# Decoder with local attention: the last tiles of gates and values share one weight tile, the order lists are rewritten, the first stage is reordered

## The chip, the cores and the metric

One NeuronCore of a Trainium2 chip. The metric is the device time of one launch in microseconds; 2953.05 us is the median of three runs of the kernel before (2951.69 to 2956.47).

## What is computed

Eight sequences of 256 tokens by 256 channels go through three blocks, all in fp32:

```python
x = x + gelu(layernorm(x) @ W_K.T @ W1.T) @ W2.T             # memory read, 64 hidden
x = x + softmax(q k.T / 16) v                                 # cross attention: q from layernorm(x), k and v from ctx
y = layernorm(x)
for i in range(6):                                            # six layers
    y = local_attention(shift(y)) @ Wo[i] + y                 # 16 heads of 64, windows of 64, rotary, l2 norms
    a, g = split(layernorm(shift(y)) @ W1[i] + b1[i])         # 682 values and 682 gates
    y = (a * gelu(g)) @ W2[i] + b2[i] + y
x = x + y
```

682 is five tiles of 128 and a rest of 42.

## The kernel before, in words

`front` does the memory read and the cross attention in two quads of four sequences. Each step of a quad is a loop over its four sequences on each engine: transposes of the normalised rows (line 443), hidden (453), read (460), keys (468), transposes again, values (478), queries (485), scores (495), transposes of the probabilities (502), cross output (508). The layer norms are DVE work with a power taken on POOL: (0, 0), (0, 1), (1, 0), (0, 2), (1, 1), (1, 2) by quad and place, (i, 2) being the last norm of a quad, whose result is the `y` that the layers read. Beside this, the weights of layer 0 are staged in six blocks (`Weights.stage`, lines 235 to 252), split by ACT into a high part (`split_high`) and by POOL into a low part (`split_low`). All loads go through SP's queue, in the order in which SP issues them. PE begins after one semaphore, `weights_in`, has counted ten loads (line 428).

`layers` runs 48 steps (6 layers by 8 sequences) as a software pipeline of slots. A slot mixes the attention of one step, the projections of the next and the feed-forward of the one before. What each engine does in a slot is written out by hand in PE_ORDER, ACT_ORDER, DVE_ORDER and POOL_ORDER (lines 66 to 97); an engine works strictly along its list and waits on semaphores. An item of PE's list is a group of matmuls: `unit` (6 matmuls 128x512, line 884), `turn` (4 or 8 transposes, 899 to 903), `project_out` (24, line 914), `norm_turn` (924), `input` (867), `gate` and `value` (12 matmuls 128x256, line 939), `down` (12, line 954), `scores` (976), `turned` (988), `mix` (1002 to 1006). Two PSUM banks `project` take the units and turns in turn, so each waits until the one before the last was read; `wide` takes gates and values, one item after the other.

Every product is three passes (high by high, low by high, high by low). `wide` holds two tiles of 128 columns by 256 tokens; gate items 0, 1, 2 fill tiles 0 to 5 of the gates and value items 0, 1, 2 tiles 0 to 5 of the values. The sixth tile of each has 42 columns that count; the other 86 are the next columns of the weight row or padding. ACT takes the gelu of the gates (line 1085), with a table load before the first and another back to exp after the last (1129). DVE multiplies values by gates (1292), ACT and DVE split the product (1094 to 1097, 1300 to 1303) and `down` uses it.

```python
for k in range(2):
    col = (2 * i + k) * P + (FFN if kind == "gate" else 0)
    for h in range(HALVES):
        for a, w in PASSES:
            last = pe.matmul(wide[:, k, :], w_up[w][:, h * W1_COLS + col:h * W1_COLS + col + P], xnT[a][:, h, :], ...)
```

The weights of the next layer are split chunk by chunk during a layer (`chunk_split_high`, `chunk_split_low`, lines 286 and 291), stored to HBM and fetched at the change of layers (line 315).

Of the kernel before, what the change touches and what calls it, by code (L numbers as in the profile page):

```python
# [4 lines left out]
FP32 = mybir.dt.float32  # L5
# [6 lines left out]
P = 128  # L12
# [20 lines left out]
W1_COLS = 2 * FFN  # L33
W1_PAD = FFN_TILES * P - FFN
# [41 lines left out]
ACT_ORDER = [  # L76
    ("out", 3), ("unit", 1, 0), ("unit", 1, 1), ("exp", 0, 0), ("exp", 0, 1), ("unit", 1, 2), ("unit", 1, 3), ("copied", 0, 0),
    ("copied", 0, 1), ("split_high", 0, 0), ("turn", 1, 0), ("turn", 1, 1), ("split_high", 0, 1), ("exp", 1, 0), ("turn", 1, 2),
    ("out", 0), ("unit", 1, 4), ("exp", 1, 1), ("unit", 1, 5), ("turn", 1, 3), ("copied", 1, 0), ("input",), ("copied", 1, 1),
    ("norm_turn",), ("exp", 2, 0), ("unit", 0, 0), ("exp", 2, 1), ("unit", 0, 1), ("gate", 0), ("copied", 2, 0), ("out", 1),  # L80
    ("unit", 0, 2), ("gate", 1), ("unit", 0, 3), ("copied", 2, 1), ("gate", 2), ("exp_table",), ("exp", 3, 0), ("value", 0),
    ("split_high", 1, 0), ("turn", 0, 0), ("split_high", 1, 1), ("unit", 0, 4), ("out", 2), ("value", 1), ("exp", 3, 1),
    ("turn", 0, 1), ("turn", 0, 2), ("value", 2), ("copied", 3, 0), ("unit", 0, 5), ("turn", 0, 3), ("copied", 3, 1),
]
DVE_ORDER = [
    ("mask", 0, 0), ("mask", 0, 1), ("out", 3), ("rotate", 1, 0), ("rotate", 1, 1), ("scale", 0, 0), ("scale", 0, 1),
    ("rotate", 1, 2), ("rotate", 1, 3), ("add_out",), ("mask", 1, 0), ("norm_stats",), ("mask", 1, 1), ("scale", 1, 0),
    ("norm_apply",), ("scale", 1, 1), ("split_low", 0, 0), ("out", 0), ("input",), ("mask", 2, 0), ("mask", 2, 1),
    ("norm_turn",), ("scale", 2, 0), ("rotate", 0, 0), ("split_low", 0, 1), ("rotate", 0, 1), ("scale", 2, 1), ("out", 1),
    ("rotate", 0, 2), ("rotate", 0, 3), ("mask", 3, 0), ("value", 0), ("low", 0), ("value", 1), ("mask", 3, 1), ("low", 1),  # L90
    ("scale", 3, 0), ("value", 2), ("scale", 3, 1), ("low", 2), ("out", 2), ("split_low", 1, 0), ("split_low", 1, 1),
    ("residual",),
# [87 lines left out]
class Weights:  # L180
# [5 lines left out]
    def __init__(self, nc, ctx, D):  # L186
# [6 lines left out]

        self.up_flat = two("w_up", [P, HALVES * W1_COLS + W1_PAD])
        self.up = [part[:, 0:HALVES * W1_COLS].rearrange("p (k n) -> p k n", k=HALVES) for part in self.up_flat]
# [19 lines left out]
    def split_views(self, blk):  # L215
# [7 lines left out]
        if blk < 5:  # L223
            pieces = []
            for a in range(0, FFN, 2 * P):
                b = min(a + 2 * P, FFN)
                at = FFN if blk == 3 else 0
                pieces.append([(s[:, :, a:b], self.up[0][:, :, at + a:at + b], self.up[1][:, :, at + a:at + b])])
            return pieces
# [1233 lines left out]
```

## Time and profile before

| what | value |
|---|---|
| median of the runs | 2953.05 us |
| the profiled execution's own time | 2952.34 us |
| its span | 2950.6 us |
| PE, DVE, ACT, POOL busy | 94%, 78%, 67%, 46% of the span |
| mean granted TensorE clock | 0.987 |
| matmuls on line 939 (gates and values) | 3456 |

The span runs from the first instruction to the last; 1.7 us of the execution's own time lie outside it. Busy shares are per engine; a matmul's recorded duration is longer than its share of the engine, since matmuls overlap, so what a group takes is read from one start to the next.

### The profile page before, as it was taken

The numbers are of one execution on the slowest core, as the hardware profiler recorded it, in microseconds if no ns is written. First come the engines' busy times: TensorE is split into PE (matmuls) and PEld (weight loads), VectorE is DVE, ScalarE is ACT, GpSimd is POOL, SyncE is SP. The second block draws the span as 40 slices with busy tenths as digits, with TensorE's granted clock in tenths as the row PEclk, the third lists the DMA queues.
The fourth block names the chain that finished last, engine by engine and source line by source line (L and its number), as shares of the span: only waits on it lengthen the run. The fifth ranks groups of instructions, "written<-read, shape, count | busy, mean of one in ns | idle before, by whom it ended". The sixth has DMA issues, their size and how long they took to land. (4 is left out here: it accounts for less than half of the span.)

```text
span 2950.6 us, 80978 instructions
## 1 busy us (share of the span) xinstructions
PE 2779.4 (94%) x26408; PEld 2447.7 (83%) x26408; DVE 2311.7 (78%) x7881; ACT 1976.5 (67%) x5719; POOL 1363.0 (46%) x1436
## 2 busy tenths in 40 slices
PE   7769999999999999999999999999999999999996
PEld 5658888888888888888888888888888888888886
DVE  3568888887888878888887888878888887887873
ACT  4346776777677667677767767766776776676663
POOL 3354453544445445454444545545454454545440
PEclk9989999999999999999999999999999999999997
DMA  3212222333322324222144232233223232210110
GB/s 121 86 36 90 75 70 88 112 100 111 106 75 70 110 96 141 84 87 81 63 140 138 71 96 76 79 130 135 77 70 103 75 135 86 65 30 23 37 25 20
DMA packets 140063, 251.67 MB, mean 85 GB/s; under 512 B 14718, under 2 KB 78728, under 8 KB 138632
## 3 DMA queue, kind: packets, MB, share of 16 engines
q1 hardware_dynamic: 139912, 249.76, 25.8%
q8 instruction: 83, 1.36, 0.2%
q14 instruction: 68, 0.56, 0.1%
HBM read 137.72 MB, written 80.55 MB: 74 GB/s over the span
## 5 line engine op out<-in xcount | busy, mean ns | idle before, releaser
L884 PE MATMUL project<-w_qkv,xT 128*128 128x512 f32 x3456 | 892.5, 402 | 17.5 <-DVE with_sin L1254 11.3
L884 PEld LDWEIGHTS project<-w_qkv,xT 128*128 128x128 f32 x3456 | 621.9, 189 | 156.6 <-issue 13.1
L1158 POOL TENSOR_SCALAR sums_sq<-sums_sq 128x8 f32<-128x8 f32 x384 | 92.1, 240 | 1241.6 <-DVE sums_sq L1249 1236.1
L1104 ACT ACTIVATE probs<-probs,shift 128x128 f32<-128x128 f32 x1536 | 595.3, 390 | 72.7 <-DVE shift L1322 72.4
L1322 DVE CUSTOM_DVE_ANT_0 probs<-score,mask,query_scale 128x128 f32<-128x128 f32 x1536 | 439.9, 348 | 157.8 <-PE score L976 146.9
L939 PE MATMUL wide<-nT,w_up 128*128 128x256 f32 x3456 | 480.4, 289 | 13.5 <-ACT gates L1085 3.4
L939 PEld LDWEIGHTS wide<-nT,w_up 128*128 128x128 f32 x3456 | 441.0, 191 | 44.4 <-ACT gates L1085 23.7
L1334 DVE TENSOR_SCALAR probs<-probs,sums 128x128 f32<-128x128 f32 x1536 | 426.6, 341 | 13.5
L1053 ACT ACTIVATE with_sin<-project 128x512 f32<-128x512 f32 x384 | 230.1, 599 | 189.6 <-PE project L884 189.5
L1167 POOL TENSOR_TENSOR sums_sq<-sums_sq,half 128x8 f32<-128x8 f32 x192 | 321.4, 1674 | 16.0
L1164 POOL TENSOR_TENSOR query_scale<-sums_sq,half 128x8 f32<-128x8 f32 x192 | 317.7, 1654 | 22.2 <-POOL sums_sq L1158 12.3
L1111 ACT COPY probsT<-turned 128x512 f32<-128x512 f32 x384 | 224.9, 586 | 135.7 <-issue 99.8
L914 PE MATMUL acc<-w_out,oT 128*128 128x256 f32 x2304 | 295.7, 284 | 1.6 <-issue 1.6
L914 PEld LDWEIGHTS acc<-w_out,oT 128*128 128x128 f32 x2304 | 285.9, 188 | 5.9 <-issue 1.7
L1104 ACT ACTIVATION_READ_ACCUMULATOR probs<-probs,shift 128x1 f32 x1536 | 288.6, 188 | 0.0
L988 PE MATMUL turned<-ident,probs 128*128 128x128 f32 x1536 | 236.9, 277 | 41.6 <-DVE probs L1334 40.3
L1249 DVE TENSOR_REDUCE sums_sq<-with_sin 128x8 f32<-128x512 f32 x384 | 260.4, 678 | 18.9 <-ACT with_sin L1053 18.2
L1254 DVE TENSOR_TENSOR with_sin<-project,tables 128x512 f32<-128x512 f32 x384 | 260.9, 680 | 0.0
L1252 DVE TENSOR_TENSOR with_cos<-project,tables 128x512 f32<-128x512 f32 x384 | 260.9, 679 | 0.0
L1170 POOL TENSOR_TENSOR with_cos<-with_cos,with_sin 128x512 f32<-128x512 f32 x192 | 249.5, 1299 | 0.0
L1292 DVE SCALAR_TENSOR_TENSOR gates<-wide,params,gates 128x256 f32<-128x256 f32 (+1 forms) x288 | 125.9, 479 | 148.8 <-PE wide L939 148.8
L954 PE MATMUL acc<-w_down,hT 128*128 128x256 f32 (+1 forms) x1728 | 236.8, 283 | 1.8 <-DVE hT L1303 1.6
(119 smaller groups left out, 4655.7 us busy)
## 6 DMA issues: line engine op xcount, KB each, us to landing
w_parts_scratch<-staging SPq DMA_DIRECT2D x120, 519.0 KB, 3.1
staging<-in_w_next SPq DMA_DIRECT2D x60, 519.0 KB, 5.0
w_qkv<-w_parts_scratch SPq DMA_DIRECT2D x20, 1536.0 KB, 9.3
v_mid<-v SPq DMA_DIRECT2D x192, 128.0 KB, 2.3
w_up<-w_parts_scratch SPq DMA_DIRECT2D x20, 682.0 KB, 6.2
y_in<-y_scratch SPq DMA_DIRECT2D x48, 256.0 KB, 3.7
res<-y_scratch SPq DMA_DIRECT2D x48, 256.0 KB, 2.8
y_scratch<-res SPq DMA_DIRECT2D x40, 256.0 KB, 4.1
```

The lines of the kernel that those rows point to most:

```text
L884: last = pe.matmul(project[(x - 1) % 2][:], xT[a][:, h, t * P:(t + 1) * P], w_qkv[w][:, h, c, g, :], start=(h == 0 and (a, w) == PASSES[0] ...
L914: last = pe.matmul(acc[:, t, :], oT[a][:, p, t * P:(t + 1) * P], w_out[w][:, p, :], start=(p == 0 and (a, w) == PASSES[0]), stop=(p == PAI ...
L939: last = pe.matmul(wide[:, k, :], w_up[w][:, h * W1_COLS + col:h * W1_COLS + col + P], xnT[a][:, h, :], start=(h == 0 and (a, w) == PASSES ...
L1104: last = act.activation(probs[:, k, cols], probs[:, k, cols], ACT.Exp, bias=shift[:, k, i:i + 1], scale=-1.0, accum_out=sums[:, k, i:i + 1])
L1164: pool.tensor_tensor(query_scale[:, u // 2, g * GROUP_HEADS:(g + 1) * GROUP_HEADS], sums_sq[:, u, :], half[:, 0:GROUP_HEADS], ALU.pow).the ...
L1167: pool.tensor_tensor(sums_sq[:, u, :], sums_sq[:, u, :], half[:, 0:GROUP_HEADS], ALU.pow)
L1170: pool.tensor_tensor(with_cos[:, u, :], with_cos[:, u, :], with_sin[:, u, :], ALU.add).then_inc(pool_step, 1)
L1249: dve.tensor_reduce(sums_sq[:, u, :], with_sin[:, u, :].rearrange("p (h d) -> p h d", h=GROUP_HEADS), AXIS_X, ALU.add).then_inc(squares_su ...
L1252: dve.tensor_tensor(heads(with_cos[:, u, :]), heads(bank[:]), table(2 * c), ALU.mult)
L1254: dve.tensor_tensor(heads(with_sin[:, u, :]), heads(bank[:])[:, :, ::-1, :], table(2 * c + 1), ALU.mult).then_inc(parts_ready, 1)
L1322: last = dve.tensor_tensor_reduce(out=probs[:, h, a:b], in0=score[h % 2][:, at + a:at + b], in1=mask[:, a:b], scale=query_scale[:, i, head ...
L1334: last = dve.tensor_scalar(probs[:, h, a:b], probs[:, h, a:b], sums[:, h, i:i + 1], None, ALU.mult)
```

## The change

Three parts.

1. The 42 rest columns of the values and of the gates are laid side by side in one tile of 128 columns of `w_up` (values at 0, gates at 64, the gaps zeroed). `gate` 2 computes gate tile 4 and this shared tile; `value` 2 computes value tile 4 alone. ACT takes the gelu of rows 64 to 105 of the shared tile; a new DVE item `rest` multiplies rows 0 to 41 of PSUM (plus bias) by it, and only then is `wide` given back to `value` 0. The rest columns are fetched by extra DMAs (42 columns each, 20 in all), and `gate` 2 now also waits for the values' weights.
2. All lists but POOL's are rewritten.
3. `front`: the loads are reordered, three of them (`ident`, `wk_mem`, `w1t_mem`) issued by ACT and waited for alone; PE's wait for the other weights, with the mask that is the last of them, comes before the read; x arrives by one semaphore for each of the first four; contexts of the second quad are loaded as soon as the values of the first are done; layer norm (1, 0) comes before the scores of the first quad; the cross sums of a quad are interleaved with the statistics of its last norm; the splits of blocks 0, 2, 3 and 5 come after an ACT step that they came before; the first `y_in` of the layers is loaded inside `front`, the tables are built after `input`, and only one column of `xT` is cleared in each part.

```diff
-W1_COLS = 2 * FFN
+FULL = FFN - FFN_REST
+GATE_REST = 64
+W1_COLS = 2 * FULL + P
...
 PE_ORDER = [
-    ("scores", 0), ("mix", 3), ("unit", 1, 0), ("unit", 1, 1), ("project_out", 0), ("unit", 1, 2), ("unit", 1, 3),
-    ("turned", 0, 0), ("project_out", 1), ("turned", 0, 1), ("turn", 1, 0), ("turn", 1, 1),
-    ("scores", 1), ("mix", 0), ("turn", 1, 2), ("unit", 1, 4), ("unit", 1, 5), ("turn", 1, 3), ("turned", 1, 0), ("norm_turn",),
-    ("input",), ("turned", 1, 1),
+    ("scores", 0), ("mix", 3), ("unit", 1, 0), ("unit", 1, 1), ("project_out", 0), ("unit", 1, 2), ("project_out", 1),
+    ("turned", 0, 0), ("unit", 1, 3), ("turned", 0, 1), ("turn", 1, 0),
+    ("scores", 1), ("mix", 0), ("turn", 1, 2), ("unit", 1, 5), ("turn", 1, 1), ("unit", 1, 4), ("turned", 1, 0), ("turn", 1, 3),
+    ("turned", 1, 1), ("input",), ("norm_turn",),
     ("scores", 2), ("mix", 1), ("unit", 0, 0), ("unit", 0, 1), ("gate", 0), ("turned", 2, 0), ("unit", 0, 2), ("gate", 1),
     ("unit", 0, 3), ("turned", 2, 1), ("gate", 2),
-    ("scores", 3), ("mix", 2), ("value", 0), ("turn", 0, 0), ("unit", 0, 4), ("value", 1), ("down", 0), ("turn", 0, 1),
-    ("turn", 0, 2), ("value", 2), ("down", 1), ("turned", 3, 0), ("unit", 0, 5), ("turn", 0, 3), ("turned", 3, 1), ("down", 2),
+    ("scores", 3), ("mix", 2), ("value", 0), ("unit", 0, 4), ("value", 1), ("turned", 3, 0), ("turn", 0, 1), ("down", 0),
+    ("unit", 0, 5), ("value", 2), ("down", 1), ("turn", 0, 0), ("turn", 0, 2), ("turned", 3, 1), ("turn", 0, 3), ("down", 2),
 ]
...
+    ("out", 3), ("unit", 1, 0), ("exp", 0, 0), ("unit", 1, 1), ("exp", 0, 1), ("unit", 1, 2), ("split_high", 0, 0),
+    ("copied", 0, 0), ("unit", 1, 3), ("copied", 0, 1), ("turn", 1, 0), ("out", 0), ("exp", 1, 0), ("turn", 1, 2),
+    ("unit", 1, 5), ("exp", 1, 1), ("turn", 1, 1), ("unit", 1, 4), ("copied", 1, 0), ("turn", 1, 3), ("input",),
+    ("copied", 1, 1), ("norm_turn",), ("exp", 2, 0), ("unit", 0, 0), ("exp", 2, 1), ("unit", 0, 1), ("gate", 0), ("out", 1),
...
+    ("rotate", 1, 2), ("add_out",), ("rotate", 1, 3), ("mask", 1, 0), ("mask", 1, 1), ("norm_stats",), ("scale", 1, 0),
+    ("split_low", 0, 0), ("scale", 1, 1), ("norm_apply",), ("out", 0), ("input",), ("mask", 2, 0), ("mask", 2, 1),
...
+    ("rotate", 0, 3), ("rest",), ("mask", 3, 0), ("mask", 3, 1), ("value", 0), ("scale", 3, 0), ("low", 0), ("value", 1),
+    ("split_low", 0, 1), ("out", 2), ("low", 1), ("scale", 3, 1), ("value", 2), ("low", 2), ("split_low", 1, 0), ("residual",),
...
             def slot(s):
-                if s.early:
+                if s.early and not (isinstance(n, int) and n == -1):
                     wait(sp, filled, n * FILLS + 2)
...
-                    for k in range(2):
-                        col = (2 * i + k) * P + (FFN if kind == "gate" else 0)
+                    for k in range(1 if x == 7 else 2):
+                        col = (2 * i + k) * P + (FULL if kind == "gate" else 0)
...
-                    last.then_inc(wide_read, 1)
+                        rows = slice(0, P) if j < FFN_TILES - 1 else slice(GATE_REST, GATE_REST + FFN_REST)
+                        last = act.activation(gates[rows, j, :], wide[rows, k, :], ACT.Gelu,
+                                              bias=params[rows, FFN_TILES + j:FFN_TILES + j + 1])
+                    last.then_inc(wide_read if i < 2 else gated, 1)
...
+                elif kind == "rest":
+                    dve.wait_ge(params_loaded, s.layer * 32 + 32)
+                    dve.wait_ge(gated, f + 1)
+                    j = FFN_TILES - 1
+                    dve.scalar_tensor_tensor(gates[0:FFN_REST, j, :], wide[0:FFN_REST, 1, :], params[0:FFN_REST, j:j + 1],
+                                             gates[GATE_REST:GATE_REST + FFN_REST, j, :], ALU.add, ALU.mult).then_inc(wide_read, 1)
```

and in `front` (PE, SP, DVE):

```diff
-            pe.wait_ge(weights_in, 16 * 10)
+            pe.wait_ge(fold_in, 16 * 3)
...
+                if i == 0:
+                    pe.wait_ge(weights_in, 16 * 7)
...
+            W.stage(sp, 0)
+            for k in range(QUAD, BATCH):
+                sp.dma_start(x[k][:], as_tiles(D["x"][k])).then_inc(x_in[QUAD], 16)
+            sp.dma_start(T["mask"][:], D["mask"]).then_inc(weights_in, 16)
+            for blk in (1, 2):
+                W.stage(sp, blk)
+            sp.wait_ge(kv_ready, 2 * QUAD)
+            for k in range(QUAD, BATCH):
                 load_context(k)
...
+                    sp.wait_ge(y_stored, 16 * QUAD)
+                    sp.dma_start(T["y_in"][:], as_tiles(D["y"][0])).then_inc(T["y_loaded"], 16)
...
+                if i == 0:
+                    layer_norm(1, 0, lambda j: dve.wait_ge(x_in[QUAD], QUAD * 16))
...
-                if i == 0:
-                    layer_norm(1, 0, lambda j: dve.wait_ge(x_in[1], QUAD * 16))
-                layer_norm(i, 2, lambda j: dve.wait_ge(cross_added, i * QUAD + j + 1))
+                    dve.wait_ge(cross_added, k + 1)
+                layer_norm(i, 2, add_cross)
```

## Rows read from the trace of the kernel before

**Rows 1.** The page: busy time of each engine over the span.
```profile
PE 2779.4 (94%) x26408; PEld 2447.7 (83%) x26408; DVE 2311.7 (78%) x7881; ACT 1976.5 (67%) x5719; POOL 1363.0 (46%) x1436
```

**Rows 2.** Busy time by stretch, one slot of layer 2 (columns in the first line).
```profile
core 0: us, PE busy (x) PEld busy (x) DVE busy (x) ACT busy (x) POOL busy (x), PEclk, DMA share, GB/s
1218.00:1274.70 56.70, 55.22 (x542) 48.83 (x541) 47.57 (x162) 40.71 (x118) 27.05 (x28) 1.00 0.25 82
```

**Rows 3.** Timeline of PE, same slot: start, duration, line, tiles, count [idle before].
```profile
1218.01 0.60 PE L867 MATMUL project<-ident,y_in 128*128 128x128 f32 x4
...
1219.03 1.10 PE L976 MATMUL score<-kT,qT 64*64 64x128 f32 x32
...
1234.82 1.69 PE L939 MATMUL wide<-nT,w_up 128*128 128x256 f32 x12
...
1242.62 1.66 PE L939 MATMUL wide<-nT,w_up 128*128 128x256 f32 x12
1244.12 1.55 PE L954 MATMUL acc<-w_down,hT 128*128 128x256 f32 x12
...
1249.92 1.10 PE L976 MATMUL score<-kT,qT 64*64 64x128 f32 x32
...
1263.85 0.60 PE L988 MATMUL turned<-ident,probs 128*128 128x128 f32 x4
...
1265.56 0.66 PE L899 MATMUL project<-ident,with_cos 128*128 128x128 f32 x4 [0.23 <-DVE with_sin L1254]
...
1271.94 0.60 PE L899 MATMUL project<-ident,with_cos 128*128 128x128 f32 x4
1273.14 0.66 PE L988 MATMUL turned<-ident,probs 128*128 128x128 f32 x4 [0.60 <-DVE probs L1334]
1274.24 0.65 PE L924 MATMUL wide<-ident,xn 128*128 128x128 f32 x4 [0.45 <-DVE xn L1277]
1274.73 0.60 PE L867 MATMUL project<-ident,y_in 128*128 128x128 f32 x4
```

**Rows 4.** Timeline of ACT, same slot: gelu of gate 2, the first exp of `scores` 1.
```profile
1232.84 0.84 ACT L1085 ACTIVATE gates<-wide,params 128x256 f32<-128x256 f32 x2 [0.78 <-PE wide L939]
...
1268.19 0.40 ACT L1104 ACTIVATE probs<-probs,shift 128x128 f32<-128x128 f32 x1 [0.83 <-DVE shift L1322]
```

**Rows 5.** Timeline of DVE, same slot: end of the last rotation, the mask behind it.
```profile
1232.94 0.68 DVE L1254 TENSOR_TENSOR with_sin<-project,tables 128x512 f32<-128x512 f32 x1
1234.13 0.35 DVE L1322 CUSTOM_DVE_ANT_0 probs<-score,mask,query_scale 128x128 f32<-128x128 f32 x1 [0.50 <-PE score L976]
...
1234.40 0.35 DVE L1322 CUSTOM_DVE_ANT_0 probs<-score,mask,query_scale 128x128 f32<-128x128 f32 x1
```

**Rows 6.** Groups by line and form, whole span: the product of the sixth tile.
```profile
L1292 DVE SCALAR_TENSOR_TENSOR gates<-wide,params,gates 42x256 f32<-42x256 f32 x48 | 22.5, 469 | 0.0
```

**Rows 7.** Timeline of PE in `front` and at the start of `layers`.
```profile
27.05 6.42 PE L460 MATMUL fb<-w2t_mem,hidT 64*128 64x256 f32 x16 [1.89 <-ACT hidT L522]
...
69.94 7.17 PE L508 MATMUL fb<-fv,fpT 128*128 128x256 f32 x32 [1.89 <-ACT fpT L553]
81.98 3.81 PE L443 MATMUL fb<-ident,xn 128*128 128x128 f32 x16 [4.87 <-DVE xn L593]
...
100.09 8.58 PE L468 MATMUL fb<-ctxT,wk_cross 128*128 128x256 f32 x32 [6.81 <-DMA ctxT<-in_ctxT]
108.50 1.91 PE L443 MATMUL fb<-ident,xn 128*128 128x128 f32 x16
...
135.29 7.17 PE L508 MATMUL fb<-fv,fpT 128*128 128x256 f32 x32 [1.46 <-ACT fpT L553]
155.94 1.09 PE L867 MATMUL project<-ident,y_in 128*128 128x128 f32 x4 [13.48 <-DMA y_in<-y_scratch]
159.02 7.23 PE L884 MATMUL project<-w_qkv,xT 128*128 128x512 f32 x18 [1.99 <-DVE xT L1231]
```

**Rows 8.** Timeline of SP's queue at the start of `layers`.
```profile
153.10 0.39 SPq L775 DMA_DIRECT2D y_in<-y_scratch  x1
```

**Rows 9.** Busy time by stretch, the first 20 us (columns as in rows 2).
```profile
0.00:20.00 20.00, 3.73 (x17) 3.51 (x18) 5.67 (x23) 1.87 (x2) 4.30 (x15) 1.00 0.90 294
```

More of the change, by code:

```diff
@@ L78 @@
[L78 to L81, printed above, removed]
@@ new lines @@
+    ("copied", 1, 1), ("norm_turn",), ("exp", 2, 0), ("unit", 0, 0), ("exp", 2, 1), ("unit", 0, 1), ("gate", 0), ("out", 1),
+    ("copied", 2, 0), ("unit", 0, 2), ("gate", 1), ("split_high", 0, 1), ("unit", 0, 3), ("copied", 2, 1), ("gate", 2),
+    ("exp_table",), ("exp", 3, 0), ("value", 0), ("exp", 3, 1), ("unit", 0, 4), ("turn", 0, 1), ("out", 2), ("value", 1),
+    ("unit", 0, 5), ("copied", 3, 0), ("value", 2), ("turn", 0, 0), ("split_high", 1, 0), ("turn", 0, 2), ("turn", 0, 3),
+    ("split_high", 1, 1), ("copied", 3, 1),
@@ L84 @@
 ]
 DVE_ORDER = [
[L86 to L90, printed above, removed]
@@ L192, in __init__ @@
         self.out = two("w_out", [P, PAIRS, DIM])
-        self.up_flat = two("w_up", [P, HALVES * W1_COLS + W1_PAD])
-        self.up = [part[:, 0:HALVES * W1_COLS].rearrange("p (k n) -> p k n", k=HALVES) for part in self.up_flat]
+        self.up = two("w_up", [P, HALVES, W1_COLS])
         self.down = two("w_down", [P, FFN_TILES, DIM])
@@ L224, in split_views @@
             pieces = []
-            for a in range(0, FFN, 2 * P):
-                b = min(a + 2 * P, FFN)
-                at = FFN if blk == 3 else 0
+            at, rest = (FULL, 2 * FULL + GATE_REST) if blk == 3 else (0, 2 * FULL)
+            for a in range(0, FULL, 2 * P):
+                b = min(a + 2 * P, FULL)
                 pieces.append([(s[:, :, a:b], self.up[0][:, :, at + a:at + b], self.up[1][:, :, at + a:at + b])])
+            pieces[-1].append((s[:, :, FULL:FFN], self.up[0][:, :, rest:rest + FFN_REST], self.up[1][:, :, rest:rest + FFN_REST]))
             return pieces
@@ L522, in _ @@
                     act.activation(hidT[j][:], bank[j][1][0:MEMORY, 0, :], ACT.Gelu).then_inc(hid_act, 1)
+                for piece in range(WEIGHT_PIECES[3 * i]):
+                    W.split_high(act, 3 * i, piece)
                 for j in range(QUAD):
@@ L553, in _ @@
                     act.copy(prT[j][:], bank[j][0][:]).then_inc(probs_out, 1)
+                for piece in range(WEIGHT_PIECES[2 + 3 * i]):
+                    W.split_high(act, 2 + 3 * i, piece)
         @block.gpsimd
@@ L623, in _, with add_cross @@
                     dve.reciprocal(rs[j][:], sm[j][:]).then_inc(inverse, 1)
-                for j in range(QUAD):
+                def add_cross(j):
                     k = i * QUAD + j
@@ L1285, in dense @@
                     dve.wait_ge(wide_filled, f * WIDE_FILLS + 5 + i)
-                    if i == 0:
-                        dve.wait_ge(params_loaded, s.layer * 32 + 32)
-                        dve.wait_ge(wide_read, f * WIDE_FILLS + 4 + 1)
-                    for k in range(2):
+                    for k in range(2 if i < 2 else 1):
                         j = 2 * i + k
-                        rows = P if j < FFN_TILES - 1 else FFN_REST
-                        last = dve.scalar_tensor_tensor(gates[0:rows, j, :], wide[0:rows, k, :], params[0:rows, j:j + 1],
-                                                        gates[0:rows, j, :], ALU.add, ALU.mult)
+                        last = dve.scalar_tensor_tensor(gates[:, j, :], wide[:, k, :], params[:, j:j + 1], gates[:, j, :],
+                                                        ALU.add, ALU.mult)
                     last.then_inc(wide_read, 1)
```

97 lines of the change are left out of this document (48 added, 49 removed).

## The prediction

> **What bounds the kernel now.** I read the page first. PE is busy for 94% of the span, DVE, the next, for 78% [rows 1]. The busy time by stretch says the same of a slot in the middle of a layer: 55.22 of 56.70 us on PE, 47.57 on DVE, 40.71 on ACT, at full clock [rows 2]. The slot's period is seen again from one `input` to the next, 1218.01 to 1274.73 [rows 3]. So in some 48 such slots, 2720 us, the columns that PE streams set the end, plus what PE waits for. The waits are larger than the idle of the page, because modelled ends cover part of them. I read them from start to start. `turn` (1, 3), four transposes, holds PE from 1271.94 to 1273.14, where four transposes with no wait behind them (the `input`, 1218.01 to about 1218.45) take 0.44: 0.76 of wait. The next group of four, 1273.14 to 1274.24, hides 0.66. From 1263.85 to 1265.56 stand four and eight transposes, some 1.27 of work: 0.44 of wait [rows 3]. That is 1.9 us a slot, all in the half between `scores` 0 and `scores` 2. The `front` is the other place: its PE timeline has holes of 1.89, 4.87, 6.81, 1.46 and 13.48 us [rows 7].
>
> **Part 1, the shared tile.** It removes 6 of the 12 matmuls of `value` 2, and nothing else on PE. `value` 2 runs from 1242.62 to 1244.12, 1.50 for 12 [rows 3]; allowing 0.09 of it for the change to the next kind of work, six are 0.71 us, and 48 times that is 34 us. They count in full only if `down` 1 behind them isn't late: in the new list `unit` (0, 5) lies between `down` 0 and `value` 2, so the split product has a whole unit (1.4 us) more. The bounds are 0 (the wait behind them takes it) and 36 us (0.75). By the Trainium skill (TensorE: Matmul & The Clock Gate, Part 1), a matmul of N columns takes N / 2.4 GHz plus about 2.5 ns, 109 ns for 256. The row has 125, so by the page the saving would be 31 us; the measurement decides.
>
> What it adds is `rest`, as long as the product that it replaces, 0.47 us [rows 6], so DVE's work stays the same, but in a new place: `value` 0 on PE now waits for gelu, then `rest`. The gelu of gate 2 runs 1232.84 to 1233.68 [rows 4]; the last rotation on DVE ends at 1233.62 [rows 5]; `rest` would run from 1233.75 to 1234.25. PE comes to `value` 0 at 1234.82, after `scores` 3 and `mix` 2 [rows 3]. Cover 0.57 us, cost 0. The mask behind it starts at 1234.3 where it had 1234.13 [rows 5]. If the cover is gone the cost is up to 0.6 a slot. Masks follow each other by 0.27 though each lasts 0.35 [rows 5], an overlap of 0.08. A wait for a drained engine before and after `rest` would cost twice that, 0.16 a slot on DVE, inside the cover, and 8 us in all without it. The Trainium skill (VectorE: DVE Perf Modes, "Two Vector instructions with no wait between them") has such a rule: an instruction whose operands start in another group of 32 partitions than those before it starts only when they have finished, and `rest` reads gates from partition 64. No row here has such an operand.
>
> The 20 extra fetches of 42 columns stand behind the last `value` 2 of a layer, a whole half slot (over 25 us) before the next gate 0: cost 0. The cover is SP's queue having nothing urgent behind them.
>
> **Part 2, the lists.** I walked the new lists with the durations of the rows. Between `scores` 2 and `value` 0, PE's list is the old one, and so is its time. From `value` 0 to `scores` 0 I find no wait on either side. From `scores` 0 to `scores` 2 the old slot takes 56.70 less the 30.89 from 1219.03 to 1249.92, so 25.81 [rows 2, 3]. In the new list the norm comes last and `turned` (1, 0) no longer waits for the statistics that wait for a DMA, so the 1.9 us go. But ACT becomes tight: the exps of `scores` 1 (1.56 us, in the old slot from 1268.19 [rows 4]) now stand behind the copy of `mix` 0, and behind them the reads that free the two banks. I find `turn` (1, 1), `unit` (1, 4), `turn` (1, 3) and `turned` (1, 1) each late by 0.3 to 0.6, and `scores` 2 at 25.4. Gain 0.4 a slot, times 47 is 19 us. Bounds: all 1.9 go (89 us); or each late read is later by one more copy (about 0.45 for three of them), 0.9 lost a slot (minus 42 us). The chunk splits only change place; the last is past the slot's end, so the next chunk loads start about 2 us later, and ACT has that much idle before it needs them: 0.
>
> **Part 3, the front.** By its steps:
> - PE's first wait falls, but the read now waits for the mask, the last of the first burst of loads. That burst is about 6.2 MB and the queue moves 294 GB/s [rows 9]: 21 us, with landing 21.5, against 27.05 [rows 7]: 5.5 gained. Bounds 0 and 8.
> - The splits of blocks 2 and 5 no longer stand before the copies of the probabilities: the 1.89 and 1.46 before the cross outputs [rows 7], 3.4 in all.
> - Norm (1, 0) is done early and the contexts are there: the 4.87 before the transposes at 81.98 and the 6.81 before the keys at 100.09 go; without a hole ahead the transposes take 1.91 instead of 3.81 [rows 7]. 13.6. What is late next is norm (1, 1), which by my walk ends about when the keys do. Bounds 6.8 and 15.
> - Sums and statistics interleaved at the end of quad 1: 2.4 (bounds 0 and 3).
> - `y_in` was issued at 153.10 [rows 8] and PE started at 155.94, its first unit at 159.02 after 1.99 of waiting for DVE, which built tables first [rows 7]. Now transposes start at about 153 and the unit at 155.5: 3.5. Bounds 0 and 5.
>
> Together 28 us, between 15 and 33.
>
> **Sum.** 2952.3 (the execution's own time, 0.7 below the median) less 34, 19 and 28 is 2871 us.
>
> **The rivals.** The forecast's own range is 2850 to 2888: the upper end is no gain from the lists at all (2890), the lower a gain of 0.8 a slot.
>
> *The lists win much more.* PE waited 1.9 us a slot; if ACT's reads come as early as PE wants them, two thirds of the remaining 1.5 go as well, 47 us, and the time is about 2824. For it: no engine but PE is near its limit [rows 2], and a chain that I find late by 0.3 to 0.6 may well be on time. Against: two banks and a strict order leave hand-offs.
>
> *ACT's chain takes back.* The late reads at `unit` (1, 4) and `turn` (1, 3) are each one copy later than I walked: 0.9 lost instead of 0.4 gained a slot, 61 us over 47 slots above the forecast, 2932. For it: the gap before the exps was already a wait for DVE (0.83) [rows 4], and the copy of `mix` 0 is now before them.
>
> *Slower: `rest` in the path.* If the last rotation ends one rotation (1.8 us) later relative to gate 2, then `rest`, the masks and `value` 0 move with it; beyond 0.57 of cover, PE waits 1.2 at `value` 0 and as much again at `turned` (3, 0), which now comes two items earlier. 2.4 a slot is 113 us, against 62 gained by columns and front, and nothing gained by the lists: 3003. It decides against the change from about 1.4 us a slot on. Against it: PE's order up to gate 2 is unchanged and one low split is taken out of DVE's list there.
>
> **How the numbers follow.** A difference of 0.2% (6 us) is about what a measurement of this kernel can tell from none. Forecast 0.45, lists win more 0.26 (2800 to 2850), ACT takes back 0.22 (2888 to 2946), no difference 0.02, slower 0.05. Faster is the sum of the first three, 0.93. The range leaves out the lower third of the second case, the upper third of the third, and the last two, about 0.2: 2823 to 2920. The likeliest value is 2871.
>
> **What would show it.** Line 939 with 3168 matmuls, none of them idle before `down` 1. `rest` in DVE's groups 48 times with about 0.47 each and no wait of PE for it at `value` 0: right; a wait of PE's wide line for DVE gates in each slot: the slower rival. The period of a slot about 55.6: right; 54.5: the lists win more; 56.5: ACT takes back, shown by PE idle for ACT's reads at lines 884 and 899. The first unit of `layers` at about 131 with the read at 21.5: right. The read at 27 or a new hole before line 443 in the second quad would make the front's term wrong.

## The result, and the profile after

| | before | after |
|---|---|---|
| median (us), 4 runs each | 2954.76 (2951.69 to 2959.06) | 3000.54 (2994.60 to 3004.68) |
| ratio, 95% interval | | 1.0152 [1.0130, 1.0175] |
| the profiled execution's own time; span | 2952.3; 2950.6 | 2999.97; 2997.9 |

The change made the kernel 1.5% slower, 46 us by the medians, where 2871 us was forecast and the range went up to 2920. 3168 matmuls on the wide line, the read at 21.3, the shared tile and the front all came as forecast or better. The loss is in the slots (the period from one `input` to the next). This is the page of after (busy time, as in [rows 1]), and one slot of the same layer (columns as in [rows 2]):

```profile
PE 2774.6 (93%) x26120; PEld 2418.5 (81%) x26120; DVE 2450.8 (82%) x7881; ACT 1995.3 (67%) x5721; POOL 1361.0 (45%) x1438
...
1251.00:1309.20 58.20, 54.88 (x537) 47.94 (x536) 50.86 (x161) 41.16 (x118) 26.97 (x28) 1.00 0.24 80
```

The slot is 58.20 us where it was 56.70, though PE has six matmuls fewer to do. DVE has the same number of instructions over the span, 7881, and is busy 139 us more. So some instructions on DVE became longer. The groups by line (busy us, mean ns of one | idle before) name them, before and after:

```profile
L1334 DVE TENSOR_SCALAR probs<-probs,sums 128x128 f32<-128x128 f32 x1536 | 426.6, 341 | 13.5
```
```profile
L1366 DVE TENSOR_SCALAR probs<-probs,sums 128x128 f32<-128x128 f32 x1536 | 565.9, 431 | 13.7 <-DVE sums L1362 0.2
...
L965 PE MATMUL wide<-nT,w_up 128*128 128x256 f32 x3168 | 450.3, 291 | 13.2 <-DVE nT L1311 2.5 <-issue 2.1 <-ACT gates L1112 2.1
...
L288 ACT CAST staging<-staging 128x519 fp32r<-128x519 f32 x120 | 75.1, 626 | 77.2 <-DMA staging<-in_w_next 77.2
```

The scaling of the probabilities (four instructions for a pair of heads) takes all of the 139 us. The second new thing is the 77.2 us that ACT waits for the chunks of the next layer's weights; before it was 3.0. PE's waits (us in total, times, longest), before and then after:

```profile
PE turned L988 <- DVE probs L1334: 40.3, 49, 2.2
PE wide L924 <- DVE xn L1277: 27.7, 47, 7.9
```
```profile
PE turned L1014 <- DVE probs L1366: 94.8, 51, 3.5
```

The wait for the norm is gone but for one of 7.8, as forecast; the one for the scaled probabilities has more than doubled. And it stands elsewhere: 37.5 of the 40.3 were at `turned` (1, 0), 87.4 of the 94.8 are at `turned` (2, 1). The timeline of one slot of after, DVE, POOL and PE around `turned` (2, 1), shows where:

```profile
1290.14 0.69 DVE L1372 TENSOR_TENSOR oT<-mix,oT 128x512 fp32r<-128x512 f32 x1 [0.53 <-ACT oT L1146]
...
1290.93 1.28 POOL L1199 TENSOR_TENSOR with_cos<-with_cos,with_sin 128x512 f32<-128x512 f32 x1
1290.95 3.98 DVE L1366 TENSOR_SCALAR probs<-probs,sums 128x128 f32<-128x128 f32 x4
...
1292.29 1.10 POOL L1202 TENSOR_TENSOR with_cos<-with_cos,sums_sq 128x512 f32<-128x512 f32 x1
1293.34 0.28 POOL L1215 MEMSET xn<- 1x128 f32 x1
1293.59 1.25 POOL L1218 TENSOR_TENSOR res<-res,b_down 128x512 f32<-128x512 f32 x1
...
1294.98 0.66 PE L1014 MATMUL turned<-ident,probs 128*128 128x128 f32 x4 [2.35 <-DVE probs L1366]
```

POOL's work here is a train of four: an addition (L1199) and a product (L1202) for the rotation, a `memset`, and the addition of the output bias (L1218). Before, the same four scalings were done just as POOL's rotation began, and took 0.88:

```profile
1228.58 0.88 DVE L1334 TENSOR_SCALAR probs<-probs,sums 128x128 f32<-128x128 f32 x4
...
1229.41 1.29 POOL L1170 TENSOR_TENSOR with_cos<-with_cos,with_sin 128x512 f32<-128x512 f32 x1
```

Read the end times: 1290.95 + 3.98 is 1294.93, and POOL's addition of the bias ends at 1294.84. The scaling ends with POOL's train, whatever its own work is. DVE's list explains the meeting: before, it had ("scale", 2, 1), ("out", 1); the new one has them the other way round, and `out` 1 (L1372, which waits 0.53 for ACT's copy and lasts 0.69) moves the scaling into POOL's train. The single instructions, from narrow windows of DVE's timeline (the first alone, the last two together, the last alone):

```profile
1290.95 1.35 DVE L1366 TENSOR_SCALAR probs<-probs,sums 128x128 f32<-128x128 f32 x1
...
1292.42 2.51 DVE L1366 TENSOR_SCALAR probs<-probs,sums 128x128 f32<-128x128 f32 x2
...
1293.40 1.53 DVE L1366 TENSOR_SCALAR probs<-probs,sums 128x128 f32<-128x128 f32 x1
```

The first ends with the rotation's addition (1292.30 and 1292.21); the second slips into POOL's pause of 0.08 us (0.27 us, as if alone); the third ends with the rotation's product (1293.48 and 1293.39); the fourth with the bias. The Trainium skill (SBUF — State Buffer, "Who interferes with whom") says that DVE and GpSimd share one pair of SBUF ports as an exclusive lock, that a `tensor_scalar` in DVE's two-port mode takes it, and that whoever issues first keeps it for the whole instruction while the other is fully blocked. These rows agree for the first three; that the scalings run in this mode is not shown by a row of its own. The powers that POOL computes on 128x8 do not keep them out: at 1228.58 before, one had been running since 1227.78 (1.71 us), and the scaling took 0.88.

The wait brings a second loss in some slots. In 10 of the 45 slots from the third on, the granted clock of TensorE fell to 0.50 (1.2 of 2.4 GHz) soon after PE had stood at `turned` (2, 1). This is a stretch of such a slot (columns as in [rows 2]):

```profile
1236.00:1238.00 2.00, 2.00 (x11) 2.00 (x10) 2.00 (x5) 0.59 (x1) 1.58 (x2) 0.50 0.00 0
```

These slots take 59.2 to 59.5 us, the other regular ones 58.2. Before, no slot had such a fall at this place.

### The profile page after: what moved, and what is told of

The parts are those of the page before. It is cut to its first block and busy times, and to the rows that moved or that the text cites. A ratio compares the mean times of both kernels' runs of the same rounds, so it can differ in the third digit from the quotient of the medians.

```text
span 2997.9 us, 80467 instructions
## 1 busy us (share of the span) xinstructions
PE 2774.6 (93%) x26120; PEld 2418.5 (81%) x26120; DVE 2450.8 (82%) x7881; ACT 1995.3 (67%) x5721; POOL 1361.0 (45%) x1438
## 5 line engine op out<-in xcount | busy, mean ns | idle before, releaser
L908 PE MATMUL project<-w_qkv,xT 128*128 128x512 f32 x3456 | 909.7, 403 | 16.5 <-DVE with_sin L1283 11.3
L1366 DVE TENSOR_SCALAR probs<-probs,sums 128x128 f32<-128x128 f32 x1536 | 565.9, 431 | 13.7 <-DVE sums L1362 0.2
L965 PE MATMUL wide<-nT,w_up 128*128 128x256 f32 x3168 | 450.3, 291 | 13.2 <-DVE nT L1311 2.5
L965 PEld LDWEIGHTS wide<-nT,w_up 128*128 128x128 f32 x3168 | 411.8, 194 | 60.6 <-ACT gates L1112 20.6
L1014 PE MATMUL turned<-ident,probs 128*128 128x128 f32 x1536 | 238.0, 278 | 129.2 <-DVE probs L1366 94.8
L1014 PEld LDWEIGHTS turned<-ident,probs 128*128 128x128 f32 x1536 | 177.8, 142 | 176.9 <-DVE probs L1366 147.3
L1199 POOL TENSOR_TENSOR with_cos<-with_cos,with_sin 128x512 f32<-128x512 f32 x192 | 248.5, 1294 | 0.0
```

Of the source, the lines that this page charges most:

```text
L908: last = pe.matmul(project[(x - 1) % 2][:], xT[a][:, h, t * P:(t + 1) * P], w_qkv[w][:, h, c, g, :], start=(h == 0 and (a, w) == PASSES[0] ...
L965: last = pe.matmul(wide[:, k, :], w_up[w][:, h, col:col + P], xnT[a][:, h, :], start=(h == 0 and (a, w) == PASSES[0]), stop=(h == HALVES - ...
L1014: last = pe.transpose(turned[:, (TILES * side + i) * P:(TILES * side + i + 1) * P], pr[:, i * P:(i + 1) * P], ident[:])
L1366: last = dve.tensor_scalar(probs[:, h, a:b], probs[:, h, a:b], sums[:, h, i:i + 1], None, ALU.mult)
```

## The experiments

**1. The exchange undone.** After, with the two DVE items back in the old order:

```diff
-    ("norm_turn",), ("scale", 2, 0), ("rotate", 0, 0), ("rotate", 0, 1), ("out", 1), ("scale", 2, 1), ("rotate", 0, 2),
+    ("norm_turn",), ("scale", 2, 0), ("rotate", 0, 0), ("rotate", 0, 1), ("scale", 2, 1), ("out", 1), ("rotate", 0, 2),
```

> The changed kernel with two neighbours in DVE's list exchanged: the scaling of the probabilities of scores 2 (second pair) stands before the split of mix 1 instead of behind it. Theory port: in the changed kernel this scaling starts in the moment in which POOL starts its three wide instructions and is held until they end (3.98 us for four instructions instead of 0.88), and PE waits 2.35 us a slot for it. One place earlier it ends before POOL starts: about 0.9 us, the slot 58.2 falls to 55.5 to 56, the time to 2880 to 2905. Rival tile: the rest product in the path of value 0 costs the time; then the exchange changes nothing beyond 10 us, 2990. Rival ACT: the order of ACT's list holds PE; then under half comes back, 2950 to 2980.

Measured: 2908.17 us, ratio 0.9841 [0.9820, 0.9863]. The slot is 56.2 instead of 58.2, and the scaling again 0.88, ahead of POOL's rotation:

```profile
1250.87 0.88 DVE L1366 TENSOR_SCALAR probs<-probs,sums 128x128 f32<-128x128 f32 x4
...
1252.08 1.30 POOL L1199 TENSOR_TENSOR with_cos<-with_cos,with_sin 128x512 f32<-128x512 f32 x1
```

Two names exchanged in a list are 92 us (1.0152 less 0.9841, times 2953): twice the whole loss. The falls of the clock behind `turned` (2, 1) are gone with the wait. Ten slots at 1.25 us each are about 12 of the 92 (an estimate from the slots of after).

**2. The exchange made in the kernel before.** The same two items, swapped the other way, nothing else.

> The kernel before with the same two neighbours exchanged the other way, nothing else. Theory port: the scaling then starts at 1229.5 on the clock of the slot that was read, POOL's wide instructions run from 1229.4 to 1233.2, so it takes about 3.9 us instead of 0.88, and PE, which wants the result at 1230.8, waits some 2.5 us in each of 46 slots: 2950 becomes 3030 to 3075. Rivals tile and ACT: neither the tile nor the lists of PE and ACT are in this kernel, so it stays within 0.6 us a slot of 2952, the length of the split that now stands ahead: at most 2980.

Measured: 3107.76 us in one run, 33 above the forecast range. PE waits 144.4 us for the probabilities instead of 40.3, and the single slot shows the same picture:

```profile
PE turned L988 <- DVE probs L1334: 144.4, 93, 2.6
```
```profile
1231.24 3.72 DVE L1334 TENSOR_SCALAR probs<-probs,sums 128x128 f32<-128x128 f32 x4
...
1235.02 0.66 PE L988 MATMUL turned<-ident,probs 128*128 128x128 f32 x4 [2.51 <-DVE probs L1334]
```

The exchange is enough by itself; no other part of the change is needed for the loss. The wait alone adds 104 of the 155 us. Most of the rest is the clock, which the forecast had left out. In 29 of the 45 slots from the third on it fell to 0.50 behind this wait (columns as in [rows 2]):

```profile
1296.50:1298.20 1.70, 1.70 (x21) 1.48 (x24) 1.51 (x3) 0.64 (x2) 1.62 (x3) 0.50 0.00 0
```

The twelve matmuls of `gate` 2 behind the wait then take 2.55 from start to start instead of 1.59, and `scores` 3 takes 1.59 instead of 1.04. Slots with the fall take 60.96, the others 59.42 (medians), about 45 us over 29 slots.

**3. The old lists.** The new tile and front, with the three lists of before and `rest` put in between ("rotate", 0, 3) and ("mask", 3, 0).

> The changed kernel (shared tile, new front) with the three lists of the kernel before; the rest product is put in DVE's list between the last rotation and the mask of scores 3. Theory port: with the old lists the scaling is ahead of POOL again, so the tile gives its 34 us and the front its 34: 2885 to 2900. Rival tile: the rest product holds value 0 in these lists too, and the time is 2920 (front alone) or above.

Measured: 2880.29 us, ratio 0.9745 [0.9720, 0.9771], slot 55.9. So what the new lists cost in all is 1.0152 less 0.9745, 120 us. In this kernel the shared tile's saving can be read (timeline of PE, six matmuls, then `down` 1):

```profile
1251.57 0.95 PE L964 MATMUL wide<-nT,w_up 128*128 128x256 f32 x6
1252.36 1.54 PE L979 MATMUL acc<-w_down,hT 128*128 128x256 f32 x12
```

0.79 from start to start, where twelve took 1.50 [rows 3]: 0.71.

**4. The first chunk split later.** k1 with ACT's ("split_high", 0, 0) moved back behind the turn:

```diff
-    ("out", 3), ("unit", 1, 0), ("exp", 0, 0), ("unit", 1, 1), ("exp", 0, 1), ("unit", 1, 2), ("split_high", 0, 0),
-    ("copied", 0, 0), ("unit", 1, 3), ("copied", 0, 1), ("turn", 1, 0), ("out", 0), ("exp", 1, 0), ("turn", 1, 2),
+    ("out", 3), ("unit", 1, 0), ("exp", 0, 0), ("unit", 1, 1), ("exp", 0, 1), ("unit", 1, 2),
+    ("copied", 0, 0), ("unit", 1, 3), ("copied", 0, 1), ("turn", 1, 0), ("split_high", 0, 0), ("out", 0), ("exp", 1, 0), ("turn", 1, 2),
```

> k1_scale_first with ACT's first staging split of the next chunk moved from its new place (behind value unit 2 of tile 1) to behind the second turn, about where it stood in the kernel before. Theory C (the loads of the next chunk are issued too early for their data, ACT waits some 2 us for them in each slot and 6 to 7 us in the first slot of each layer, and everything behind it on ACT with it): ACT's wait for staging falls from 73.7 us to under 20, the first slots of a layer fall from 61.3 to 62.9 to about 57, the regular slot from 56.2 to about 55.6; time 2860 to 2880. Rival (the long first slots come from somewhere else, and the split is merely what ACT stands at): the wait goes elsewhere and the time stays at 2900 to 2915.

Measured: 2883.16 us, ratio 0.9758 [0.9724, 0.9792]. ACT's wait for staging fell from 73.7 to 3.2 us.

In the slots that had been long, one in each layer from the second to the fifth, the time fell from between 61.3 and 62.9 to between 56.0 and 56.5, together worth 25 us. In k1 PE stood about 4 us for ACT at `turned` (0, 1) in each of them (15.4 us in four places), and the granted clock fell to 0.50 behind it; in k4 neither is there. But the regular slot stayed at 56.2: the 2 us that ACT waited in each were beside PE's work, and only the long waits at the start of a layer were in its path. In the last layer, which loads no chunks, the slot is 55.3, where k3 has 55.8. The rest of a regular slot is another collision (timeline of DVE, POOL and PE, unit (3, 0)):

```profile
1197.33 2.19 DVE L1366 TENSOR_SCALAR probs<-probs,sums 128x128 f32<-128x128 f32 x4
...
1199.58 0.66 PE L1014 MATMUL turned<-ident,probs 128*128 128x128 f32 x4 [0.53 <-DVE probs L1366]
```

**5. A shorter train on POOL.** After, with the bias added to 8 columns of each tile; it leaves out the bias of all other columns.

> The changed kernel with POOL's addition of the output bias narrowed to 8 columns of each tile; this leaves out the bias for all other columns. Port theory (the scaling of value unit (2,1) can't run while POOL's train of two-input additions runs, and ends as soon as that ends): the train is shorter by about 1.1 us, so the scaling of (2,1) takes about 2.8 us instead of 3.98, PE's wait at the turn of its products falls from 2.35 to about 1.2 us, the regular slot from 58.2 to about 57.1, time 2940 to 2955. Rival (the scaling is late for its operands, by the order of DVE's list alone, and POOL only happens to be busy): nothing changes in the 3.98 us, and the time stays at 2995 to 3005.

Measured: 2939.23 us in one run, slot 56.9. The numbers of the port theory came (2.8, 1.2 and 57.1 were expected), and the time is 1 us below its range:

```profile
1265.19 2.81 DVE L1366 TENSOR_SCALAR probs<-probs,sums 128x128 f32<-128x128 f32 x4
...
1268.06 0.66 PE L1014 MATMUL turned<-ident,probs 128*128 128x128 f32 x4 [1.13 <-DVE probs L1366]
```

DVE's list is that of after. Only POOL's work was cut, by 1.04 us a slot (the bias takes 0.21 instead of 1.25), and DVE's scaling became 1.17 shorter and the slot 1.2. So the scaling isn't late for its operands; POOL keeps it out.

**6. One instruction instead of four.** After, with

```diff
-                for h in (2 * j, 2 * j + 1):
-                    for i, (a, b) in enumerate(((0, P), (P, BAND))):
-                        last = dve.tensor_scalar(probs[:, h, a:b], probs[:, h, a:b], sums[:, h, i:i + 1], None, ALU.mult)
-                    last.then_inc(probs_scaled, 1)
+                view = probs[:, pair, :].rearrange("p h (i c) -> p h i c", i=TILES)
+                dve.tensor_tensor(view, view, sums[:, pair, :].unsqueeze(3).broadcast_to([P, 2, TILES, P]), ALU.mult).then_inc(probs_scaled, 2)
```

> The changed kernel with the four scalings of a unit (one tensor_scalar each of 128x128 with its own column of sums) made one product of two SBUF tensors of 128x512, the sums broadcast. Theory M (only the four operations with one tensor operand are kept out by POOL's additions): the product takes 0.65 to 0.75 us everywhere, PE's wait at the turn of unit (2,1) goes, the slot falls from 58.2 to about 55.5, time 2870 to 2900. Rival (any DVE operation that reads two SBUF tensors is kept out too, or slowed, by POOL's reads): the product beside the additions takes 2 us or more, PE still waits 1 us or more there, time 2960 to 3000.

Measured: 2899.29 us, ratio 0.9818 [0.9783, 0.9853]: the time of the first theory, by a mechanism that is half the rival's. At the same place:

```profile
1189.60 1.30 POOL L1199 TENSOR_TENSOR with_cos<-with_cos,with_sin 128x512 f32<-128x512 f32 x1
1189.80 1.64 DVE L1365 TENSOR_TENSOR probs<-probs,sums 128x512 f32<-128x512 f32 x1
...
1190.97 1.37 POOL L1202 TENSOR_TENSOR with_cos<-with_cos,sums_sq 128x512 f32<-128x512 f32 x1
...
1191.50 0.66 PE L1014 MATMUL turned<-ident,probs 128*128 128x128 f32 x4
```

The product takes 1.64 where one with nothing beside it takes 0.69, so it is kept out too. But it is kept out once, until the rotation's addition ends (1190.90), and then it is POOL's product that is held (1.37 where 1.04 to 1.10 is usual). PE doesn't wait. The same section of the Trainium skill has this rule too: a DVE instruction with two SBUF inputs contends with a GpSimd instruction that reads SBUF. The trace agrees. By these rows, four short instructions queue up for the port four times, one long one once.

**7. A collision off the path.** k4 with ("scale", 0, 0) ahead of the second rotation.

> k4_split_later with DVE's scaling of value unit (0,0) moved ahead to between the two rotations of the other half, away from POOL's additions. Theory (the collision that the kernel before has too, 2.7 us at the scaling of (0,1), costs nothing since PE has other work there): same time as k4_split_later within 0.3%, though fewer scalings last over 2 us. Rival (it delays the tail of each slot): the slot falls by 0.5 us or more, time 20 to 40 us below k4_split_later.

Measured: 2884.24 us beside 2883.16 of k4 on the same chip, slot 56.2 in both: no difference. DVE's busy time fell by 89 us, from 2367.9 to 2279.3, and none of it reached PE.

**8. k4 and the product together.**

> k4_split_later with the scalings of a unit as one product of 128x512 (as in k6_one_product). Theory (one instruction can be kept out by POOL once, four of them four times; what k4 still loses in slots with chunks is PE's wait for the scaling of unit (3,0), 2.19 us beside POOL's additions): PE's wait for the scaled probabilities falls from 31.0 us to under 8, the regular slot from 56.2 to about 55.6, time 2855 to 2870. Rival (that wait only covers another one of the same length): regular slot 56.0 or more, 2875 to 2885.

Measured: 2862.89 us, ratio 0.9696 [0.9681, 0.9711], slot 55.7. The theory held: PE's wait for the scaled probabilities fell from 31.0 to 5.6 us. What is left of the new lists' own waits in each slot:

```profile
PE project L923 <- ACT qT L1092: 19.2, 48, 0.7
PE turned L1014 <- ACT probsT L1139: 18.2, 48, 0.4
```

**9. The old lists and the product.**

> k3_old_lists with the scalings of a unit as one product. Theory (with the old lists the one scaling that stands beside POOL's additions is off PE's path): the slot stays at 55.7 to 55.9, time 2868 to 2882, within 0.4% of k3_old_lists. Rival (the held scaling delays DVE's rotations and by them PE): slot 55.3 or less, time under 2860.

Measured: 2830.04 us, ratio 0.9583 [0.9567, 0.9599]: the best kernel of this study, better than before and after, and 48 us below k3 (0.9745 less 0.9583). I had expected no difference; the rival was right, and by more than it said. The waits of PE in k3, then in k9:

```profile
PE turned L1013 <- DVE probs L1365: 35.1, 49, 2.1
PE wide L947 <- DVE xn L1305: 27.6, 47, 7.8
PE project L907 <- DVE with_sin L1282: 17.3, 51, 1.5
PE project L922 <- DVE with_sin L1282: 10.8, 47, 0.3
```
```profile
PE wide L947 <- DVE xn L1305: 23.9, 45, 7.8
PE project L907 <- DVE with_sin L1282: 9.3, 11, 1.5
PE turned L1013 <- DVE probs L1364: 8.9, 14, 1.6
```

The sum goes from 90.8 to 42.1. In k3, as in the kernel before, the scaling of (0, 1) lasts 2.71 us beside POOL, and PE doesn't wait at `turned` (0, 1). It waits much later. In the slot of each that was read, k3's rotations start 1.5 us later than k9's, counted from the slot's start, and its statistics 1.0 later. About half of the gain is at `turned` (1, 0), where PE's wait for the probabilities fell from 32.0 to 8.4 us. In k9 the product comes to the port first in 31 of 48 slots, and POOL is the one that waits (1.77 instead of 1.30), and PE does not wait for it:

```profile
1243.67 0.69 DVE L1364 TENSOR_TENSOR probs<-probs,sums 128x512 f32<-128x512 f32 x1
...
1243.75 1.77 POOL L1198 TENSOR_TENSOR with_cos<-with_cos,with_sin 128x512 f32<-128x512 f32 x1
```

In these slots the product is ahead by 0.04 to 0.08 us. In 16 of the other 17 POOL's addition is ahead by 0.02 to 0.05, and the product takes about 1.8 and the addition 1.29. Two things are not told apart in the 48 us: the holds, and that the product is 0.19 shorter than four scalings where nothing is beside it, eight times a slot. In the last layer of k4 and k8, where only the second is left on PE's path, the slot is 55.3 in both; with the old lists it was not tried.

Removing the same collision in k7 gave nothing, probably because the new lists had already put the norm behind everything else. A collision "off the path" is off the path of one list only.

**10. The front alone**, with the old tile and lists.

> The kernel before with the changed front alone (its loads, the order of its norms and splits, y_in loaded inside it, tables built after input); old tile, old lists. Theory (the two parts add up): input of the first slot at about 122 instead of 156, slots 56.7 as before, time 34 us under the kernel before, 2915 to 2925; the rest of what k3_old_lists gains, some 38 to 40 us, is then the shared tile's. Rival (the layers' first chunks of weights come no earlier, so the first slots give the start back): 2930 to 2950.

Measured: 2917.68 us, ratio 0.9877 [0.9861, 0.9893], first input at 122.06, slots 56.7. The front is 36 us, and the shared tile 0.9877 less 0.9745, 39 us.

**11. The bias in two halves.**

> The changed kernel with POOL's addition of the output bias as two instructions of 128x256 instead of one of 128x512. Theory, hold by instruction (each of the four scalings is kept out until the one POOL instruction ends beside which it stands, and is let in between two): the fourth scaling is let in after the first half, so the four last about 3.3 us instead of 3.98, PE's wait at the turn of unit (2,1) falls from 2.35 to about 1.7, the slot from 58.2 to about 57.6, time 2965 to 2980. Rival, hold by train (DVE is kept out until POOL's additions are all done): the four last 4.0 us or a little more, slot 58.2 to 58.4, time 2995 to 3010.

Measured: 3005.42 us in one run, slot 58.3. The rival's numbers came, not mine:

```profile
1295.43 1.67 DVE L1367 TENSOR_SCALAR probs<-probs,sums 128x128 f32<-128x128 f32 x1
...
1295.62 0.71 POOL L1218 TENSOR_TENSOR res<-res,b_down 128x256 f32<-128x256 f32 x1
1296.30 0.71 POOL L1219 TENSOR_TENSOR res<-res,b_down 128x256 f32<-128x256 f32 x1
...
1297.15 0.66 PE L1014 MATMUL turned<-ident,probs 128*128 128x128 f32 x4 [2.43 <-DVE probs L1367]
```

The fourth scaling was not let in between the two halves, which follow each other without a pause (the second starts 0.03 before the first's end is shown). It ended at 1297.10, after both. Here the measurement goes further than the Trainium skill's "for the whole instruction" (SBUF — State Buffer, "Who interferes with whom"): POOL instructions back to back keep DVE out together, and DVE gets in where POOL pauses.

**12. The norm later.** k9 with ("norm_turn",) behind ("input",) and ("turned", 1, 1) on PE, an idea of the new list.

> k9_old_lists_product with one thing of the new PE list: the transposes of the norm come behind the input and the second turn of unit pair 1 instead of ahead of them (some 1.1 us later). In k9_old_lists_product PE waits 23.9 us in 45 places for DVE's norm there, 0.36 to 0.5 us a slot, while the units and turns behind are ready. Theory (that wait is on PE's path and its cover is now the input and the turn): the wait goes, the slot falls from 54.8 to about 54.4, time 15 to 24 us lower, 2806 to 2818. Rival (ACT reads the input and the turned products in its list before the norm anyway, and scores 2 waits for what ACT reads): the wait turns up at the next thing, slot 54.7 to 54.9, time 2825 to 2835.

Measured: 2849.03 us, ratio 0.9651 [0.9628, 0.9675]: slower than k9 by 0.7%, slot 55.3 instead of 54.8. Beyond what the rival said:

```profile
PE project L890 <- ACT v L1082: 15.3, 38, 0.5
```

The wait for the norm went and one for ACT's read of the bank of `input` took its place, with more behind it. The norm's wait had probably been time in which ACT caught up.

## Why the prediction was wrong

**The step that failed** is this sentence of part 2: "Between `scores` 2 and `value` 0, PE's list is the old one, and so is its time." PE's list there is the old one, but DVE's is not, and `turned` (2, 1) waits for DVE: PE stands there for 87.4 us where it had no wait, because POOL's train keeps DVE's four scalings out (3.98 us instead of 0.88). I did not walk this stretch. A walk with durations from before could not have found it either without a second look, since four scalings at this place took 0.88 there. The trace of before had the warning in it: one group of four in each slot, (0, 1), lasted 2.7 us instead of 0.88, beside POOL instructions of the same lines. Where an operation has two durations in one trace, as here, look for the neighbour that sets which one it gets. Price: 92 us (k1). About 12 of them are a cost that the prediction put at nothing by counting every slot at full clock.

**The second term** is the chunk splits: "ACT has that much idle before it needs them: 0". I weighed the split that moved back, not the one that moved ahead. ("split_high", 0, 0) now comes three items earlier in ACT's list, and ACT stands there until its data has landed. 25 us (k4); the 2 us in each regular slot cost nothing, the longer ones in one slot of a layer did, the fall of the clock behind them included.

**The third** is "From `value` 0 to `scores` 0 I find no wait on either side". In k4, where the first two are mended, PE waits 28.8 us in 41 slots at `turned` (3, 0) for a scaling that POOL holds (2.2 us). The slot is 56.2 there and 55.3 in the last layer, where this scaling takes 0.88.

**The gain of 0.4 a slot** that was forecast for the half between `scores` 0 and `scores` 2 was met only where none of the three faults acts, in the last layer: k1 and k4 take 55.3 and k3 55.8. The norm's wait went, and of ACT's late reads that I had counted two are there, 0.40 at `turn` (1, 1) and 0.38 at `turned` (1, 1) (means of k8). But over all its slots k4 is no faster than k3 (0.9758 and 0.9745). And the agreement in the last layer is in part luck, since the old lists of k3 carry a hold of their own, at (0, 1). With the product in both, k8 (new lists) is at 0.9696 and k9 (old lists) at 0.9583. So the new lists are 33 us slower than the old ones once most of the holds are gone.

**Part 1 was right.** 0.71 us a slot was forecast, and 0.71 a slot for six matmuls is what k3 shows, by the row of 0.125 a matmul. By the 0.109 of the Trainium skill (TensorE: Matmul & The Clock Gate, Part 1) it would have been 0.65; the measurement stands. Over the whole kernel it is 39 us where 34 was forecast, 0.8 a slot, within the error of the two ratios. `rest` cost nothing where I put its cover: k3's PE never waits for it at `value` 0 in regular slots. In k3 it lasts 0.476 us, with its gates in other partitions, where the product that it replaces took 0.469 [rows 6]. The hand-over behind it is what changed. In after and in k3 the instruction behind `rest` starts 0.51 us after it, 0.03 after its end, while what followed the product that it replaces started after 0.39, 0.08 before its end (medians). In after, `rest` also starts 0.03 after the end of the rotation in front of it (timeline of DVE, after):

```profile
1298.54 0.48 DVE L1317 SCALAR_TENSOR_TENSOR gates<-wide,params,gates 42x256 f32<-42x256 f32 x1
1299.05 0.35 DVE L1354 CUSTOM_DVE_ANT_0 probs<-score,mask,query_scale 128x128 f32<-128x128 f32 x1
```

So these rows agree with the rule of the Trainium skill that I had weighed (VectorE: DVE Perf Modes, "Two Vector instructions with no wait between them"). The 0.11 behind `rest` is between 5 and 6 us on DVE in all, inside the cover.

**The front** gave 34.1 us at the first input and 35.0 at the first unit (123.98 for 159.02), where 28 was forecast. The hole terms were nearly right: the read at 21.34 for 21.5, and 6.2 instead of 5.9 in the tail from the last cross output to the first unit. The range of 15 to 33 was no plain sum of the bounds of its steps, which gives 10 to 34. What was missing stands in durations of groups (timeline of PE, after, beside [rows 7]):

```profile
21.34 3.72 PE L479 MATMUL fb<-w2t_mem,hidT 64*128 64x256 f32 x16 [0.46 <-DMA mask<-in_mask]
24.98 7.17 PE L487 MATMUL fb<-ctxT,wk_cross 128*128 128x256 f32 x32
...
121.82 1.09 PE L891 MATMUL project<-ident,y_in 128*128 128x128 f32 x4 [8.19 <-POOL xT L1175]
```

The read took 6.42 before and 3.72 now, the first keys 9.49 and 7.17, the second 8.58 and 7.17: some 6.4 from start to start. A view that puts 16 matmuls in one row hides the waits between them in its length. I had noticed that for the transposes and not for these.

**The rivals.** "Slower" had 0.05 and named `rest`, 3003 us, at DVE's hand-over in the same half of the slot. The time was nearly that, by chance; the mechanism was not. That rival was priced with its cover, and I had no rival at all for a DVE instruction that becomes longer by where it stands. "ACT takes back" was there in kind (k8, k12), inside the 0.4.

| term | forecast (us) | measured (us) | from |
|---|---|---|---|
| shared tile | -34 | -39 | k3 and k10 |
| front | -28 | -36 | k10 |
| lists: exchange of `scale` and `out` | 0 | +92 | after and k1 |
| lists: first split too early | 0 | +25 | k4 and k1 |
| lists: all else | -19 | +4 | k4 and k3 |
| sum | -81 | +46 | |

Each measured term is a difference of two ratios times 2953; with intervals of about 0.3% each, those on the split and the tile are good to some 10 us, and the last one can't be told from zero.

## What to carry to other kernels

Where an order is written by hand, walk every engine's list, not only that of the bottleneck: ask of each moved DVE instruction which POOL instructions will run beside it, and look in the trace for an operation with two durations before using its mean. In these rows a port shared by two engines is paid for by the number of instructions that have to come to it and not only by their length: one product for four scalings was worth 48 us with the old lists (k3 to k9) and 99 with the changed ones (after to k6). A wait of PE can cost more than its length: look at the granted clock behind it (k2, 1.5 us more in each of 29 slots). A wait that is taken away is only a gain if the next engine in the row is ready: with the norm moved, PE waited for ACT's read (k12).

## What the runs showed of the hardware

- Four scalings of 128x128 in SBUF take 0.88 us alone, 2.2 to 2.8 beside two POOL instructions of 128x512 with two inputs (medians by place) and 3.98 beside three. In most slots they end 0.1 to 0.3 us after the last POOL instruction that kept them out.
- The hold lasts over POOL instructions that follow without a pause (1.67 us over a `memset` and two additions in k11, a single run); in a pause of 0.08 us one scaling gets in.
- A product of two SBUF tensors is kept out as well (1.64 instead of 0.69), once. Who comes first wins: in k9, with the product 0.07 ahead, it took 0.69 and POOL's addition 1.77; with the addition 0.02 ahead, it took 1.29 and the product 1.82.
- After PE had stood 2.5 us, its granted clock fell from 1.00 to 0.50 in 29 of 45 slots of k2; after 2.3 us, in 10 of 45 slots of after; at this place in none of the kernel before, where PE had no such wait. Twelve matmuls of 256 columns then took 2.55 us from start to start instead of 1.59.
- POOL's powers of 128x8 (1.67 us each) didn't hold the scaling. Whether it is their size or their kind was not tried.
- Whether a scaling that reads its products from PSUM would escape was not tried either.
